# A bound on the row gathers of a graph kernel, and skipped rows for empty places

## What is computed

```python
# attention: 53125 edges (row = src, col = dst), 4 heads of 64
h  = (layernorm(x) @ W).reshape(n, 4, 64)
e  = leaky_relu(hl[row] + hr[col], 0.2)          # hl, hr: one number per node and head
ee = exp(e - segment_max(e, row)[row])
out_h = segment_sum(ee / segment_sum(ee, row)[row] * h[col], row)
# relational: 4 relations, one weight matrix each
msgs[i] = x[src[i]] @ rel_W[edge_type[i]]
agg  = segment_sum(msgs, dst);  deg = clip(segment_sum(1, dst), 1)
relu(x @ self_W + self_b + agg / deg)
```

## Time and profile before

| | us |
|---|---|
| median of three runs | 1883.29 (1882.06 to 1884.16) |
| span of the profiled execution, first to last instruction | 1879.7 |
| attention gathers, first to last on POOL | 229.2 to 816.4 |
| relational gathers, first to last on POOL | 1104.3 to 1654.0 |

### The profile page before, as it was taken

How to read it: one execution, slowest core, us unless ns; L and a number is a source line. 1 busy time by engine, 2 the same in 40 slices (tenths; PEclk the granted TensorE clock), 3 DMA queues, 4 the chain that set the end, 5 groups by cost and what they waited for, 6 DMA issues and landing times.

```text
span 1879.7 us, 23044 instructions
## 1 busy us (share of the span) xinstructions
PE 1421.9 (76%) x6382; PEld 962.6 (51%) x6382; DVE 1234.0 (66%) x2879; ACT 608.8 (32%) x1757; POOL 1319.1 (70%) x1331
## 2 busy tenths in 40 slices
PE   5566567778888888679999966666666667786993
PEld 3333245655665555558876434444334333375992
DVE  6999977788898887868524125454444444477655
ACT  0688511136666665143332310000000000025435
POOL 0688677777777777768886747777777777714566
PEclk9799778889999999889999988988977776756996
DMA  5011144445544444310202574333333333305456
GB/s 98 10 30 32 19 106 108 107 104 134 143 121 118 122 117 107 107 44 10 58 2 66 140 227 114 107 105 106 106 104 106 105 106 106 104 26 147 149 154 187
DMA packets 110954, 186.08 MB, mean 99 GB/s; under 512 B 31578, under 2 KB 78125, under 8 KB 110701
## 3 DMA queue, kind: packets, MB, share of 16 engines
q0 software_dynamic: 56480, 134.84, 28.0%
q1 hardware_dynamic: 54349, 49.75, 9.4%
HBM read 152.80 MB, written 31.43 MB: 98 GB/s over the span
## 4 chain that ended last, share of the span: by engine, by line
POOL 37%; PE 23%; DVE 19%; issue 13%; DMA 8%; DVEq 0%; ACT 0%; POOLq 0%; SPq 0%; ACTq 0%
POOL gath L946 30%; PE ps L992 6%; DVE hot_c L675 6%; DMA gath<-y_tab,index_b 6%; POOL slot_tab_b L771 5%; PE ps L1482 4%; PE ps L1920 3%; PE ps L1931 3%; DVE hot_r L666 2%; DMA gath<-h_tab,index_a 2%; DVE acc L982 1%; DVE gath L1031 1%; PE ps L1656 1%; DVE hot L970 1%; POOL acc L1236 1%
## 5 line engine op out<-in xcount | busy, mean ns | idle before, releaser
L992 PE MATMUL ps<-gath,hot 128*125 128x260 f32 (+1 forms) x1808 | 595.4, 469 | 297.5 <-DVE gath L1031 99.1
L992 PEld LDWEIGHTS ps<-gath,hot 128*125 128x125 f32 x1808 | 364.3, 221 | 487.4 <-DMA gath<-y_tab,index_b 196.3
L946 POOL DMA_INDIRECT gath<-h_tab,index_a x464 | 446.2, 962 | 146.8 <-issue 136.2
L946 POOL DMA_INDIRECT gath<-y_tab,index_b x440 | 416.0, 945 | 154.9 <-issue 119.4
L982 DVE TENSOR_TENSOR acc<-acc,ps 125x257 f32 (+1 forms) x672 | 284.5, 423 | 316.6 <-PE ps L992 277.7
L716 PE MATMUL ps<-hot_c,pay 125*128 125x440 f16 (+1 forms) x901 | 194.6, 367 | 61.6 <-ACT pay L699 61.6
L771 POOL DMA_INDIRECT slot_tab_b<-sent_word_b,sent_to_b x136 | 167.7, 1233 | 36.3 <-issue 36.3
L761 POOL DMA_INDIRECT slot_tab<-sent_word,sent_to x102 | 130.2, 1277 | 81.7 <-DVE sent_to L514 50.9
L699 ACT ACTIVATE pay<-hot_r,plan_b 125x128 f16<-125x128 f16 x578 | 172.0, 386 | 0.0
L716 PEld LDWEIGHTS ps<-hot_c,pay 125*128 125x128 f16 x901 | 87.5, 100 | 160.6 <-ACT pay L699 81.5
L1031 DVE TENSOR_TENSOR gath<-gath,ps 128x1024 f32<-128x1024 f32 x116 | 136.0, 1214 | 0.0
(11 more groups left out here) (360 smaller groups left out, 2034.4 us busy)
## 6 DMA issues: line engine op xcount, KB each, us to landing
y_tab<-ybuf SPq DMA_DIRECT2D x25, 448.0 KB
y_slots<-y_buf SPq DMA_DIRECT2D x64, 128.0 KB, 1.9
gath<-h_tab,index_a POOLq DMA_INDIRECT x464, 2.8
gath<-y_tab,index_b POOLq DMA_INDIRECT x440, 2.8
h_tab<-hbuf SPq DMA_DIRECT2D x25, 113.8 KB
xa<-in_x SPq DMA_DIRECT2D x1, 2800.0 KB
xa<-in_x SPq DMA_DIRECT2D x5, 560.0 KB
xn_tab<-acc SPq DMA_DIRECT2D x5, 560.0 KB
```

Of the source, the lines that this page charges most:

```text
L946: p.indirect_dma_start(gath[:, ring(k) + s, 0:width], None, table, bass.IndirectOffsetOnAxis(ap=index[g][:, col:col + 1], axis=0)).then_in ...
L992: ins = t.matmul(sum_p(g, q, width), hot[:, s, :], gath[:, s, 0:width], start=(e == 0), stop=(e == n - 1))
```

## The change

Both aggregations' gathers now carry `bounds_check` with the last row of their table, and `oob_is_err=False`: for an index over the bound nothing is copied, so the place in `gath` keeps what it held. `mark_empty` takes the place of `spread_tail`. It adds 2^20 to the index of every empty place of the columns from 48 on (`SKIPS_FROM` is 6 groups), behind group 1, and POOL waits for it at group 6. The first six groups still read row 0 for their empty places. From column 48 on there are in "a" 22 part filled and 36 empty columns with 5903 empty places, in "b" 22 and 14 with 3087.

As a skipped place keeps old data, `gath` is filled with zeros once, in `setup_pool`. And in the attention one more DVE instruction per group takes the smaller of both scores before the slope, so that an old hr can't make the exponent positive.

```diff
-TAIL = E // 128 // GRP
+SKIPS_FROM = 6
+NOWHERE = float(1 << 20)
...
         p.memset(hrl[:, :, :], -3.0e38).then_inc(pool_ready, 1)
+        p.memset(gath[:, :, :], 0.0).then_inc(rows_blank, 1)
...
     def gather_group(p, k, table, width, g):
         per = GRP * 128 // unit[g]
-        if k == TAIL:
-            p.wait_ge(tail_spread, words[g])
+        if k == SKIPS_FROM:
+            p.wait_ge(empty_marked, words[g])
+        last = {"a": N, "b": REL * N}[g] - 1
...
-                                     bass.IndirectOffsetOnAxis(ap=index[g][:, col:col + 1], axis=0)
-                                     ).then_inc(s_gath[ring(k) + s], 16)
+                                     bass.IndirectOffsetOnAxis(ap=index[g][:, col:col + 1], axis=0),
+                                     bounds_check=last, oob_is_err=False).then_inc(s_gath[ring(k) + s], 16)
...
+        p.wait_ge(rows_blank, 1)
         for k in range(GROUPS):
             gather_group(p, k, h_tab, AW, "a")
...
-    def spread_tail(v, g):
-        at = slice(GRP * TAIL, cols[g])
-        rows = {"a": hi_s.bitcast(I32), "b": high_b}[g][:, 0:cols[g] - GRP * TAIL]
-        v.tensor_scalar(rows, local[g][:, at], 0.0, away[:, 0:1], ALU.is_lt, ALU.mult).then_inc(vector_step, vn.up())
+    def mark_empty(v, g):
+        at = slice(GRP * SKIPS_FROM, cols[g])
+        rows = {"a": hi_s.bitcast(I32), "b": high_b}[g][:, 0:cols[g] - GRP * SKIPS_FROM]
+        v.tensor_scalar(rows, local[g][:, at], 0.0, NOWHERE, ALU.is_lt, ALU.mult).then_inc(vector_step, vn.up())
...
+            v.wait_ge(vector_step, vn.n)
+            v.tensor_tensor(score[:, g, 0, :], score[:, g, 0, :], score[:, g, 1, :], ALU.min).then_inc(vector_step, vn.up())
             v.wait_ge(vector_step, vn.n)
             v.scalar_tensor_tensor(score[:, g, :, :], ..., SLOPE, ..., ALU.mult, ALU.max).then_inc(vector_step, vn.up())
...
-            if k == DEEP:
-                spread_tail(v, "a")
+            if k == 1:
+                mark_empty(v, "a")
...
-            if k == NT:
-                spread_tail(v, "b")
+            if k == 1:
+                mark_empty(v, "b")
```

More of the change, by code:

```diff
@@ L308, in build @@
     ends_turned, reach_ready, reach_summed = sem("ends_turned"), sem("reach_ready"), sem("reach_summed")
-    planned, slots_ready, tail_spread = sem("sorts_planned"), sem("slots_ready"), sem("tail_spread")
+    planned, slots_ready, empty_marked = sem("sorts_planned"), sem("slots_ready"), sem("empty_marked")
     var_ready, root_done, norm_ready = sem("var_ready"), sem("root_done"), sem("norm_ready")
@@ L321, in build @@
     s_gath = sems("gathered", RING)
+    rows_blank = sem("rows_blank")
     hot_ready, hot_turned, hot_copied = sem("hot_ready"), sem("hot_turned"), sem("hot_copied")
@@ L955, in attention_pool @@
             p.wait_ge(rows_stored[u], STORE * SETS)
+        p.wait_ge(rows_blank, 1)
         for k in range(GROUPS):
             gather_group(p, k, h_tab, AW, "a")
-    def spread_tail(v, g):
-        at = slice(GRP * TAIL, cols[g])
-        rows = {"a": hi_s.bitcast(I32), "b": high_b}[g][:, 0:cols[g] - GRP * TAIL]
-        v.tensor_scalar(rows, local[g][:, at], 0.0, away[:, 0:1], ALU.is_lt, ALU.mult).then_inc(vector_step, vn.up())
+    def mark_empty(v, g):
+        at = slice(GRP * SKIPS_FROM, cols[g])
+        rows = {"a": hi_s.bitcast(I32), "b": high_b}[g][:, 0:cols[g] - GRP * SKIPS_FROM]
+        v.tensor_scalar(rows, local[g][:, at], 0.0, NOWHERE, ALU.is_lt, ALU.mult).then_inc(vector_step, vn.up())
         v.wait_ge(vector_step, vn.n)
-        v.tensor_tensor(index[g][:, at], index[g][:, at], rows, ALU.add).then_inc(tail_spread, 1)
+        v.tensor_tensor(index[g][:, at], index[g][:, at], rows, ALU.add).then_inc(empty_marked, 1)
     def one_hots(v, k, g, ready):
```

## The result

The median of the changed kernel is 1931.2 us (1927.1 to 1932.4), that of the kernel before, run beside it, 1882.9 us. The ratio is 1.025, with a 95% interval of 1.0238 to 1.0262. The forecast was 1888.3 us. The time lies inside the range of 1846 to 1978, near the rival that prices the bound (1942.5), and 43 us above the forecast.

The account below looks back on a forecast made before the run. POOL's rate of gathers, one per 1.25 us, was taken to set 1135 us of the 1880. Memset 5.0, minimum 0.2, landing -0.2, bound 0 and skip 0 summed to +5.0 us: 1888.3 us, range 1846 to 1978.

Parts of the forecast that it names:

- the rival that prices the bound: All 904 gathers on POOL: the bound costs 0.06 us in each, 54 us, giving 1942.5 us; chance 0.30.
- What bounds the kernel: Both gather stages: POOL's period of 0.946 + 0.30 = 1.25 us per gather sets 1135 us of the 1880.
- Part 1, the move: POOL's sequencer: one more register move per gather, taken at nothing, hidden under the gather before.
- Part 1, the bound: Inside each of 904 gathers: comparing 128 indices with a bound, taken at zero, between zero and 0.24 us.
- The first rival: All 904 gathers on POOL: the bound costs time in each, priced at 0.06 us, 1942.5 us; chance 0.30.
- Part 2, skipped rows: 94 of 904 gathers: skipping saves POOL nothing; shorter landings gain 0.1 us at each stage's end, 0.2 us together.
- Part 3, the memset: Setup: POOL's memset of gath, 5.29 us, holds DVE's marks and delays PE's first matmul; taken at 5.0 us.
- three candidates: DVE's marks in setup that the memset might hold: L420 pushed by 5.36 us, L422 by 5.1, L424 by 4.85.
- Part 4: DVE's additions: the minimum costs 0.2 us in the last attention group; marking is off the path, POOL's group-6 wait met early.
- The sum: Whole kernel: 5.0 (memset) + 0.2 (minimum) - 0.2 (landing) + 0 (bound) + 0 (skip) = +5.0 us, median 1888.3 us.
- the two rivals: Gathers: the bound costs time in each (1942.5 us, chance 0.30), or skipping shortens them (1855.1 us, chance 0.30).
- What would show it: List of trace signs: gather median and gaps, minima in empty columns, a held DVE instruction, PE's first matmul, first gathers' starts.

Follow-up runs that it names:

- e8: Kernel before with the bound on all gathers and oob_is_err=True, no index over it; 1939.0 us in a single run, kernel before 1880.0.
- e3: Kernel before plus the bound on all gathers, its register loaded once per stage; 2157.1 against 2173.1 us, ratio 0.992, slow chip.
- e11: Repeat of e3 on the third chip, also slow; 2162.8 against 2174.1 us for the kernel before, ratio 0.9931.
- e2: Kernel before with a register move written ahead of each gather, no bound; the trace has no moves; 2172.5 against 2173.1 us, ratio 1.0004.
- e7: Changed kernel with the memset later and bound and marking only from column 408 on (88 gathers); 1881.7 against 1880.0 us for the kernel before, ratio 1.0007.
- e1: Kernel before plus the bound and a register move on every gather, no index over it; 2196.5 against 2173.1 us, ratio 1.0106, slow chip.
- e5: Changed kernel with every place from column 48 on skipped, so 808 of 904 gathers move no row; 1927.8 us in a single run.
- e6: Changed kernel with the memset moved behind DVE's marks by one wait; 1922.3 against 1880.0 us for the kernel before, ratio 1.0225.
- e12: Kernel before with the old spreading for all columns from 48 on, behind group 1, no bound; 2175.7 against 2174.1 us, ratio 1.0007, slow chip.
- e9: Repeat of e1 on the third chip, also slow; 2197.6 against 2174.1 us for the kernel before, ratio 1.0096.

## Why the prediction was right in sign and range, and 43 us off in its time

- **What bounds the kernel: right.** POOL's period sets both stages. The surplus per period arrived in full in the relational stage (22.8 us due and 23.0 found, in e8 29.0 and 28.8) and but for 3.1 us in the attention.
- **Part 1, the move: right for this kernel and chip.** Taken at nothing. The idle time in front of a gather is 0.305 us with the moves as without them, and e3 and e11 show the longer instruction with only two moves. The run made to show it, e2, had no moves in it, and on the slow chips the moves go with 35 to 39 us that stay open.
- **Part 1, the bound: this step failed.** The term was mis-sized: taken at 0 between bounds of 0 and 0.24 us, it is 0.052 us, 47.0 us in sum. The reason given was that gathers of 260 and of 256 numbers last equally long. That shows that the time doesn't go by the bytes of a row; it says nothing on what a further option of the instruction costs. The other reason, that a sequencer instruction is free, was about another unit: what the sequencer does nine gathers ahead is hidden (e7), what POOL does inside the gather is not. The first rival's price of 0.06 us, a quarter of the way to the scatter, was 8 ns too high. Its chance should have been above the forecast's: only an exact zero spares the kernel, and the prediction itself noted that 4 ns decide.
- The Trainium skill spoke on the same side. From its GPSIMD Engine Reference (Performance pitfalls for Q7 kernels) the prediction estimated 85 ns for a further read command. e1 and e3 show 52 to 56 ns, so the direction holds and the size is below the estimate. No run shows which part of the instruction takes the time.
- **Part 2, skipped rows: right on POOL, a little low at the landing.** Nothing by rows, and e5 extends that from 94 gathers to 808. The landing gain was put at 0.1 us per stage, at most 0.2. The attention's end after, in order of time, answers to the earlier trace rows:

```profile
842.00 1.00 POOL L950 DMA_INDIRECT gath<-h_tab,index_a  x1 [0.30 <-issue]
...
844.25 0.19 DVE L1020 TENSOR_TENSOR score<-hle,gath 128x32 f32<-128x32 f32 x1 [2.13 <-DMA gath<-h_tab,index_a]
844.48 0.19 DVE L1023 TENSOR_TENSOR score<-score 128x32 f32<-128x32 f32 x1
844.71 0.23 DVE L1025 SCALAR_TENSOR_TENSOR score<-score 128x64 f32<-128x64 f32 x1
844.97 0.19 DVE L1028 TENSOR_TENSOR expo<-score 128x32 f32<-128x32 f32 x1
```

  From the last gather's start to DVE it is 2.25 us, against 2.88 before: 0.63 gained, with the 52 ns already in it. The scatter of the earlier trace rows moves data, if little, and so was no lower bound for a transfer that moves none; e5's landing of 2.1 us is.
- **Part 3, the memset: right**, in size and place. Setup after, in order of time, answers to the earlier trace rows:

```profile
4.13 0.26 POOL L391 MEMSET hrl<- 128x200 f32 x1
4.17 5.54 DVE L422 CAST above_b<-before 128x128 bf16<-128x128 f32 x1 [4.17 <-POOL a_bd L390]
4.31 5.46 DVE L423 TENSOR_SCALAR mark_b<-ident 128x128 bf16<-128x128 f32 x1
4.33 5.29 POOL L392 MEMSET gath<- 128x6240 f32 x1
9.80 0.22 DVE L425 TENSOR_TENSOR mark_b<-mark_b,above_b 128x128 bf16<-128x128 bf16 x1
...
18.90 0.43 PE L470 MATMUL ps<-acc,ones_b 125*1 125x325 bf16 x1 [18.90 <-DVE acc L437]
```

  The memset lasts the 5.29 us that were scaled from its twin. The held instructions are a cast and the tensor-scalar behind it, both started ahead of the memset; the latter (L420 in the kernel before) was the first of the three candidates, with 5.36 us. The next instruction starts 5.24 us later than before (9.80 against 4.56) and PE's first matmul 5.19 us later (18.90 against 13.71). 5.0 had been taken. The Trainium skill's SBUF — State Buffer (Who interferes with whom), by which L422 of before passes, wasn't put to the test: that instruction came up only when the memset was over. e6 adds that the memset held none of the three reductions and the statistics that ran beside it.
- **Part 4: right.** The minimum is a step of 0.23 us in the last group (844.48 to 844.71). The marking ended at about 268 us, 29 us ahead of POOL's group 6, and e12 finds no cost in it, within its noise.
- **The sum:** 5.2 + 47.0 + 0.2, less 0.6 and 0.5 at the two landings (the relational stage's last gather starts 3.98 us ahead of DVE's first step behind its sums instead of 4.53), makes 51.3 against 48.3 in the medians (45.6 between the two profiled spans). DVE's first step behind the relational sums, after and before:

```profile
1705.61 0.18 DVE L1693 TENSOR_SCALAR s<-acc 125x25 f32<-125x25 f32 x1
...
1657.63 0.18 DVE L1686 TENSOR_SCALAR s<-acc 125x25 f32<-125x25 f32 x1
```

  The 3.1 us of fewer long gathers in the attention and the spread behind the last stage cover what is left between sum and spans.
- **The sign and the range owe something to luck.** The forecast's plus sign came from the memset, 5 of 48 us; nine tenths of the loss are the term that it put at nothing. The range held because it had been widened for the two rivals.
- **What would show it** was the right list: its first line named the rise of the gathers' median, times 904, as decisive, and that line alone told the story. By its last line, "wrong if POOL's period changes at all", the mechanism forecast is wrong: the period went from 1.25 to 1.30 us.

## What to carry to other kernels

Where POOL issues indirect DMAs back to back and nothing else is late, the stage costs count times length, and an option that costs 52 ns in the instruction costs that in each: give a bound only to instructions that need it. Making such transfers smaller or empty gives no time back on POOL (e5); by count times length only fewer instructions would, which no run here tries. A constant written once by POOL belongs where DVE does no work that a memset holds, even if POOL itself has all the time in the world.

## What the runs showed of the hardware

- A gather of 128 rows with a bound occupies POOL 998 to 1002 ns instead of 946 to 949, whatever share of its rows is over the bound (e1, e3, e5); with error reporting on and no row over it, 1012 (e8).
- A skipped row leaves the number of packets as it was (56480 in three kernels) and removes its bytes; a gather with nothing to move lands in 2.1 us instead of 2.8 at the median.
- A long memset of POOL also held DVE instructions that had started up to 0.16 us ahead of it (4.17 against 4.33), to its end.
- POOL's sequencer reached a register move 11.5 us ahead of the gather that it was for (e7).
- On two slower chips, 902 register moves ahead of bounded gathers went with 39.4 and 34.8 us (e1 less e3, e9 less e11), unexplained; on the fast chip the gaps in front of the gathers stayed as they were.
- The same kernel took 1880, 2173 and 2174 us on three chips with POOL's gathers equally long to within 4 ns and the first one starting at 229.1 to 230.0 us where there is no memset or bound (before, e2, e12); what differed came behind it, in waits whose cause those traces don't record.
